# VectorE's order in batch 0, and batch 6's last norm on GpSimd in pieces: one change to a fused attention, feed-forward and gating kernel

## The reference

```python
xn = layernorm(x)
# attention branch
q, k, v = split(xn @ Wqkv + bqkv)
qp, kp  = elu(q) + 1, elu(k) + 1
attn    = (qp @ (kp.T @ v)) / (qp . sum(kp) + 1e-6)
x1 = layernorm(xn + attn) * g1 + b1
s  = layernorm(x1 + (silu(x1 @ Wg + bg) * (x1 @ Wu + bu)) @ Wd + bd) * g2 + b2
# gate branch: three cycles of  out = out + coupling(out) * twist(out)
# coupling: a net of 128-128-64-32-1 with gelu, and one global net on the mean of xn
g  = silu(three cycles on xn)
result = x + s * g
```

## Time and profile before

| what | us |
|---|---|
| median of 3 runs | 166.69 (165.75 to 167.46) |
| the profiled execution | 166.28 |
| its span, first to last instruction | 164.4 |
| busy: TensorE / weight loads | 153.9 / 118.3 |
| busy: VectorE / ScalarE / GpSimd | 138.1 / 132.0 / 111.9 |

### The profile page before, as it was taken

How to read it: one execution, slowest core, us unless ns; L and a number is a source line. 1 busy time by engine, 2 the same in 40 slices (tenths; PEclk the granted TensorE clock), 3 DMA queues, 4 the chain that set the end, 5 groups by cost and what they waited for, 6 DMA issues and landing times.

```text
span 164.4 us, 3402 instructions
## 1 busy us (share of the span) xinstructions
PE 153.9 (94%) x934; PEld 118.3 (72%) x934; DVE 138.1 (84%) x550; ACT 132.0 (80%) x345; POOL 111.9 (68%) x197
## 2 busy tenths in 40 slices
PE   7979999999999999999999999999999999999910
PEld 7757888888898686545554655788888888888910
DVE  2888599899988989299999959968749999969892
ACT  4889876999999988999999986994568887653950
POOL 0075966789991869992084396389999998794352
PEclk9999999999999999999999999999999999999995
DMA  5997333030330000000000000000001011010113
GB/s 173 234 395 161 64 66 68 0 66 7 63 64 0 2 2 4 0 0 0 4 0 0 4 4 0 0 0 4 0 0 66 0 64 63 6 66 0 64 64 128
DMA packets 11922, 7.83 MB, mean 48 GB/s; under 512 B 8960, under 2 KB 9728, under 8 KB 11904
## 3 DMA queue, kind: packets, MB, share of 16 engines
q1 hardware_dynamic: 11616, 7.55, 16.4%
q10 hardware_dynamic: 288, 0.08, 0.2%
HBM read 3.43 MB, written 2.10 MB: 34 GB/s over the span
## 4 chain that ended last, share of the span: by engine, by line
PE 75%; ACT 9%; DVE 8%; POOL 3%; issue 3%; DVEq 0%; ACTq 0%
PE bank L1055 11%; PE bank L1247 10%; PE bank L1172 7%; PE bank L1236 7%; PE bank L1238 7%; PE bank L1237 7%; PE bank L1184 4%; PE bank L1197 4%; PE bank L1126 2%; PE bank L1137 2%; PE bank L1072 2%; PE bank L1113 2%; PE bank L1117 2%; PE bank L1114 2%; DVE u L710 2%
## 5 line engine op out<-in xcount | busy, mean ns | idle before, releaser
L505 ACT ACTIVATE pq<-bank,bffn 128x512 f32<-128x512 f32 (+1 forms) x24 | 16.1, 683 | 11.4 <-PE bank L1238 11.3
L273 POOL TENSOR_TENSOR rstd<-ve,minus_half 128x4 f32<-128x4 f32 x21 | 21.2, 1011 | 1.8
L800 DVE SCALAR_TENSOR_TENSOR pq<-bank,bffn,pq 128x512 f32<-128x512 f32 (+1 forms) x24 | 17.6, 738 | 4.8 <-issue 1.9
L1236 PE MATMUL bank<-x_hi,ffn_hi 128*128 128x512 f32 (+1 forms) x48 | 20.5, 427 | 0.0
L1237 PE MATMUL bank<-x_lo,ffn_hi 128*128 128x512 f32 (+1 forms) x48 | 18.9, 394 | 0.0
L1238 PE MATMUL bank<-x_hi,ffn_lo 128*128 128x512 f32 (+1 forms) x48 | 18.9, 394 | 0.0
L1247 PEld LDWEIGHTS bank<-wd,pq 128*128 128x128 f32 x144 | 17.9, 191 | 1.2
L1247 PE MATMUL bank<-wd,pq 128*128 128x128 f32 x144 | 18.0, 274 | 0.0
L445 ACT ACTIVATE q_stage<-bank,col 128x512 f32<-128x512 f32 x24 | 16.0, 677 | 0.4 <-PE bank L1055 0.3
L271 POOL TENSOR_SCALAR nm<-mv 128x4 f32<-128x4 f32 x21 | 4.7, 223 | 16.5 <-DVE mv L637 16.3
L327 POOL TENSOR_TENSOR ab<-cpl 128x8 f32<-128x8 f32 x4 | 6.5, 1632 | 12.3 <-ACT cpl L477 12.2
(11 more groups left out here) (173 smaller groups left out, 458.2 us busy)
## 6 DMA issues: line engine op xcount, KB each, us to landing
x_tok<-in_x SPq DMA_DIRECT2D x8, 256.0 KB, 6.5
tx_tok<-xn_tok SPq DMA_DIRECT2D x16, 128.0 KB, 2.3
out<-pq SPq DMA_DIRECT2D x7, 256.0 KB, 2.0
r_tok<-in_w_ffn SPq DMA_DIRECT2D x1, 341.0 KB, 6.4
r_tok<-in_w_first SPq DMA_DIRECT2D x1, 320.0 KB, 3.3
out<-pq SPq DMA_DIRECT2D x2, 128.0 KB, 1.9
row<-in_rows SPq DMA_DIRECT2D x1, 192.0 KB, 5.9
wd<-in_w_down SPq DMA_DIRECT2D x1, 192.0 KB, 6.4
```

Of the source, the lines that this page charges most:

```text
L273: return pool.tensor_tensor(rstd[i][:, b], ve[i][:, b], minus_half[:], ALU.pow)
L505: act.activation(sg[n % 2][0:m], gate_of(n)[0:m], ACT.Silu, bias=bffn[0:m, c:c + 1]).then_inc(sg_ready, 1)
L800: dve.scalar_tensor_tensor(out=hid[b % 2][0:m, c], in0=up_of(n)[0:m], scalar=bffn[0:m, CHUNKS + c:CHUNKS + c + 1], in1=sg[n % 2][0:m], op0 ...
L1236: pe.matmul(dst[0:m], ffn_hi[:, w], x1_hi[:, b], start=True, stop=False)
```

## The change

It does six things.

1. VectorE, batch 0: three tiles of batch 2's statistics come first, then `feature_q(0)`, the first `feature_k`, the fourth tile, and the aggregation. The copies and column instructions, now in `small_columns`, stand behind the second `feature_k`.
2. 1/std of batch 6 is no longer made by ScalarE's root and VectorE's reciprocal and product (`rstd_6` is gone) but by GpSimd's power, as for the other batches.
3. ScalarE runs `norm_2(5)` ahead of the silu of the last chunk, and the first root of batch 7 ahead of `norm_2(6)`.
4. `norm_2(6)` signals after tiles 0, 1 and 3.
5. GpSimd's product of batch 6 is made for tile 0, tile 1 and then tiles 2 and 3 together, its sum by halves.
6. The store of batch 6 moves from SyncE to the end of ScalarE's list.

The diff, cut to its core:

```diff
-            b = BATCHES - 2
-            sp.wait_ge(y_ready, b + 1)
-            sp.dma_start(out_dram[b], yb[b % 2]).then_inc(y_stored[b % 2], 16)
...
-            for b in (BATCHES - 3, BATCHES - 2):
-                multiply_rows(b)
-                add_rows_to(b)
+            b = BATCHES - 3
+            pool.wait_ge(y_ready, b)
+            pool.wait_ge(mn_ready, BATCHES)
+            pool.wait_ge(y_stored[b % 2], 16 * (b // 2))
+            link(multiply_rows(b, range(TILES), b + 1))
+            add_rows_to(b, range(TILES)).then_inc(y_ready, 1)
+            rstd_of(2, b + 1)
+            b = BATCHES - 2
+            pool.wait_ge(y_stored[b % 2], 16 * (b // 2))
+            multiply_rows(b, (0,), b + 1)
+            link(multiply_rows(b, (1,), b + 2))
+            add_rows_to(b, HALVES[0]).then_inc(y6_half, 1)
+            link(multiply_rows(b, HALVES[1], b + 3))
+            add_rows_to(b, HALVES[1]).then_inc(y_ready, 1)
...
             def norm_2(b):
-                if b == BATCHES - 2:
-                    act.wait_ge(late_ready, 1)
-                else:
-                    act.wait_ge(rstd_ready[2], b + 1)
+                act.wait_ge(rstd_ready[2], b + 1)
...
+                    if b == BATCHES - 2 and t < 2:
+                        last.then_inc(un_ready, 1)
...
+                if b == BATCHES - 1:
+                    norm_2(b - 2)
                 silu_gate(CHUNKS * b + 2)
...
-                if b >= 2:
+                if 2 <= b < BATCHES - 1:
                     norm_2(b - 2)
...
-            root(BATCHES - 2, range(TILES), 0)
+            root(BATCHES - 1, HALVES[0], 0)
             norm_2(BATCHES - 2)
-            for half, tiles in enumerate(HALVES):
-                root(BATCHES - 1, tiles, half)
+            root(BATCHES - 1, HALVES[1], 1)
+            b = BATCHES - 2
+            act.wait_ge(y6_half, 1)
+            act.wait_ge(y_ready, b + 1)
+            act.dma_start(out_dram[b], yb[b % 2]).then_inc(y_stored[b % 2], 16)
...
-            measure_part(2, HALVES[0])
+            measure_part(2, (0, 1, 2))
...
                 if b == 0:
-                    measure_part(2, (2,))
+                    measure_part(2, (3,)).then_inc(st_ready[0], 1)
+                    moments(0, 2)
...
                 if b == 0:
-                    measure_part(2, (3,)).then_inc(st_ready[0], 1)
+                    small_columns()
...
             residual_last(0)
-            rstd_6()
             measure_last(0)
```

More of the change, by code:

```diff
@@ L206, in gated_block @@
         g_ready, mn_ready, y_ready = sem("g_ready"), sem("mn_ready"), sem("y_ready")
-        y_last, multiplied, root_ready, late_ready = [
-            sem(n) for n in ("y_last", "multiplied", "root_ready", "late_ready")]
+        y_last, y6_half, root_ready, late_ready = [
+            sem(n) for n in ("y_last", "y6_half", "root_ready", "late_ready")]
         y_stored = [sem("y_stored0"), sem("y_stored1")]
@@ L284, in rstd_of, with multiply_rows, add_rows_to @@
                 pool.tensor_tensor(nmr[i][:, b], nm[i][:, b], rstd[i][:, b], ALU.mult).then_inc(rstd_ready[i], 1)
[L286 to L297, removed]
+            def multiply_rows(b, tiles, wanted):
+                pool.wait_ge(un_ready, wanted)
+                ts = slice(tiles[0], tiles[-1] + 1)
+                return pool.tensor_tensor(yb[b % 2][:, ts], un[b % 2][:, ts], tx_tok[:, b, ts], ALU.mult)
+            def add_rows_to(b, tiles):
+                ts = slice(tiles[0], tiles[-1] + 1)
+                return pool.tensor_tensor(yb[b % 2][:, ts], yb[b % 2][:, ts], x_tok[:, b, ts], ALU.add)
             def norm_x1(b):
@@ L828, in residual_6 @@
                     last.then_inc(st_ready[2], 1)
[L830 to L835, removed]
             def rstd_last(half):
@@ L840, in rstd_last @@
                 ts = slice(tiles[0], tiles[-1] + 1)
-                dve.wait_ge(root_ready, 2 + half)
+                dve.wait_ge(root_ready, 1 + half)
                 dve.reciprocal(rstd[2][:, b, ts], std[:, b % 2, ts]).then_inc(late_ready, 1)
@@ L882, in finish_last @@
                 dve.wait_ge(centred, half + 1)
-                dve.wait_ge(late_ready, 2 + half)
+                dve.wait_ge(late_ready, 1 + half)
                 for t in HALVES[half]:
@@ L896, in bias_rows, with small_columns @@
                 last.then_inc(mix_ready, 1)
+            def small_columns():
+                bias_rows()
+                dve.tensor_scalar(half_b4[:], col[:, COL["cn_b4"]:COL["cn_b4"] + 1], 0.5, None, ALU.mult)
+                dve.tensor_scalar(half_gb3[:], col[:, COL["gc_b3"]:COL["gc_b3"] + 1], 0.5, None, ALU.mult)
+                dve.tensor_scalar(gain[:, 0:1], col[:, COL["range"]:COL["range"] + 1], W_GLOBAL, None, ALU.mult)
+                dve.tensor_scalar(gain[:, 1:2], col[:, COL["range"]:COL["range"] + 1], W_TOKEN, None,
+                                  ALU.mult).then_inc(cols_ready, 1)
             def add_rows():
@@ L967, in _ @@
                 if b == 0:
-                    moments(0, 2)
                     lo_x(1)
```

## The result

The changed kernel took 165.22 us (median of 20 runs, 164.82 to 166.44) beside 166.38 us for the one before. The ratio is 0.9942 with a 95% interval of 0.9924 to 0.996: by the ratio 0.97 us less (0.67 to 1.26), where 0.65 was forecast. (The two medians by themselves are 1.16 us apart.) The profiled execution took 165.06 us with a span of 163.2, against 166.28 and 164.4.

What follows compares the result with a forecast made beforehand. TensorE was taken to bound the kernel nearly everywhere except the start and the last 10 us. Head 0.3 plus tail 0.35 gave 0.65 us off, 165.63 or 166.04, so 165.8 was forecast, range 164.9 to 166.9.

Steps and rivals of the forecast that it cites:

- Head: Batch 0's new VectorE order lets TensorE reach batch 2's transposes earlier: 0.3 us gain, bounds 0.45 and a loss of 0.1.
- what is late next is kf of tile 5: Behind batch 2's transposes, TensorE would wait for VectorE's kf of tile 5, losing 0.1 us of the head's gain.
- Travels to the end whole: From the head to 152 us everything hangs on TensorE or its followers, so 0.3 us should reach the end.
- The late silu costs VectorE's row 0.23: Tail: norm of batch 5 first makes the last silu 0.77 us late, costing VectorE's row 0.23.
- rstd leaves VectorE: Tail: without batch 6's rstd 0.95 us goes from VectorE, so its row ends 0.72 earlier net.
- GpSimd takes 1.83 us for the power: Tail: GpSimd makes batch 6's rstd in 1.83 us, so batch 6's norm starts 0.6 us late.
- The pieces: Tail: GpSimd's five pieces for batch 6 cost 0.46 us per 128 columns and 0.73 per 256.
- The store: Tail: batch 6's store, issued by ScalarE, lands at 163.57 against 163.92 for the last landing before; gain 0.35 us.
- Rival (1): GpSimd's pieces are cheap and kf doesn't hold: head 0.4, tail 0.95, 1.35 us off, 165.1; chance 0.12.
- Rival (2): The head gives nothing, kf or ScalarE's copies already setting the pace: 0.35 us off, 166.1; chance 0.18.
- Rival (3): Slower: GpSimd's five pieces and batch 6's store set the end, one piece held 1.4 us: 167.2; chance 0.10.
- the sum would stay as it is: Tail: the new order has no contending VectorE and GpSimd pair, and this was said to leave the 0.65 us unchanged.

Runs made afterwards that it cites:

- e7: Kernel before with batch 2's statistics moved forward in batch 0, but copies and column instructions left ahead of them: ratio 0.9984.
- e1: Kernel before with only VectorE's new order in batch 0, the tail unchanged: ratio 0.997.
- e3: Changed kernel with 1/std of batch 6 again by ScalarE's root and VectorE's reciprocal and product: ratio 0.9914 to the kernel before.
- e2: Changed kernel with batch 0's VectorE order put back, all edits of the tail kept: ratio 0.996 to the kernel before.
- e6: Changed kernel with batch 6's store issued by SyncE again, between the two half stores of batch 7: ratio 0.9979 to the kernel before.
- e9: Kernel before with one edit, the norm of batch 5 ahead of the last silu: ratio 0.9957.
- e4: Changed kernel with the norm of batch 5 put back behind the last silu: ratio 1.0034 to the kernel before.
- e11: Changed kernel with batch 6's 1/std by root and reciprocal, run a second time: ratio 0.9864 to the kernel before.

## Why the prediction was right, and where it was not

The direction, the range and both places were right; the size was 0.65 us for a measured 0.97 (0.67 to 1.26 by the interval), 0.94 by the profile. The range, 164.9 to 166.9, proves little: the 166.38 of the kernel before lies in it too. It is the terms that tell.

- *Head, 0.3 us forecast, 0.42 measured.* The failed step is "what is late next is kf of tile 5". TensorE sums tile n - 2 in the step of tile n, so the load at 18.17 was that of tile 4, whose kf VectorE had begun at 16.75 and so had long written (the row of before is below this list). There was nothing to wait for, and the bound of 0.45 was nearly reached. The cover named for the columns was there; that moving them bought nothing, as e7 shows, the working did not say.
- *Travels to the end whole.* Right: 0.40 at the transposes of e1, 0.44 at its last silu.
- *The late silu costs VectorE's row 0.23.* Too high. I count from the silu before the last (148.73 after; 149.47 before, at the same moment as L271 in the earlier trace rows). The hidden product starts 4.18 behind it instead of 3.50, which is 0.68 later, near the 0.77 of the working. But L833 starts 4.84 behind it (153.57 - 148.73) instead of 4.77 (154.24 - 149.47): it waited for TensorE before, and that wait took up the rest. Cost: 0.07.
- *rstd leaves VectorE, "0.95 us goes".* The size on VectorE's row was right in sum (its last step is 0.78 earlier), the cause was wrong. I booked 0.72 us net to the move of the rstd. e3 shows that with the two instructions back the row ends only 0.05 later. From batch 7's first residual to its statistics were 1.48 us before (157.05 - 155.57), 0.74 in e3 and 0.52 in the changed kernel. Of the 0.96 that went, 0.59 was L834's wait for GpSimd (0.75 against 0.16), and 0.15 was the wait of the reciprocal for a root that came late (from the residual to the reciprocal were 0.59 us before, 156.16 - 155.57, and 0.44 in e3, 155.06 - 154.62). The early norm takes both away by itself. Only 0.22 belongs to the two instructions, and half of that fits into a wait for TensorE. The contention itself I had read correctly, and I had even written that GpSimd's rows of batch 5 would be over by 155.7, but I did not draw the consequence that the root would then have been cheap where it was.
- *GpSimd takes 1.83 us for the power; norm of batch 6 0.6 us later.* Right as a time for the power: 155.01 to 156.84 is 1.83. The norm came 0.45 later (156.87 - 148.73 = 8.14 behind the silu before the last, against 7.69), since the late silu cost less. But the power is a price, and the comparison that matters is with a root that finds GpSimd idle: from the start of batch 6's aggregation to its norm are 2.33 us in the changed kernel (156.87 - 154.54) and 1.15 in e3 (155.47 - 154.32). Of these 1.18 us the differences in the table show 0.58 to 0.68 at the end.
- *The pieces.* 0.46 and 0.73 from the line between 4 and 512 columns; measured 0.454, 0.722 and 0.724 on average. The last piece ended at 160.66, which is 11.93 us behind the silu before the last, against 12.07 in the working (161.54 - 149.47).
- *The store.* Forecast gain of the tail 0.35, measured 0.43 at the last landing (163.92 - 149.47 = 14.45 behind the silu before the last, and 162.75 - 148.73 = 14.02) and 0.52 in e2's difference. The mechanism is e6's: the place in SyncE's queue.

The row of before for the first of these points, from its timeline of VectorE:

```profile
16.75 0.28 DVE L687 SCALAR_TENSOR_TENSOR kf<-ek,bank 128x128 f32<-128x128 f32 x1
```

Rival (1) had kf not holding, which came, but not its cheap pieces. Rival (2) fell with e1. Rival (3) fell with the rows: no piece was held in any of the seven profiles that have pieces. The rule of the Trainium skill ("SBUF — State Buffer", Who interferes with whom), that a VectorE instruction with two SBUF inputs contends with a GpSimd instruction that reads SBUF, is borne out: 0.75 us (before) and 0.76 (e1) beside a GpSimd sum, 0.16 and 0.16 (e3, e9) without one. I had said that by this rule "the sum would stay as it is". It did not: the 0.59 us of the pair are more than the 0.52 that the whole tail gained.

What stays open: what the stops at the start are (last section), and whether the kernels have a part in them. It was not tried. The changed kernel alone gave 8.83 and 9.08 for its first projection.

## What to carry to other kernels

When a tiny instruction is long in a trace, look first for the neighbour that ends when it ends, and price the edit that moves the neighbour away by itself: here two moved lines (0.68 us) did as much as the rewritten tail (0.52), and undoing one part of the rewrite gained another 0.6. Compare a new way of making a value with the old one as it would run after the other edits, not as it ran before them. Time saved on an engine counts only to the next wait it has in common with another engine. To know which tile a load belongs to, count the loop's lag, not the row's position.

## What the runs showed of the hardware

The start scatters more than the change is worth, and the scatter has a row. In e4 TensorE's weight loads of the first weights stand still three times for 0.30 or 0.31 us, and a fourth time for 0.18, with "issue" as the reason, that is, waiting for nothing that the profile shows. In e11 there is no such stop:

```profile
4.84 0.50 PEld L1064 LDWEIGHTS bank<-r_tok 128*128 128x128 f32 x2 [0.31 <-issue]
...
6.50 0.34 PEld L1068 LDWEIGHTS bank<-r_tok 128*128 128x128 f32 x1 [0.30 <-issue]
7.14 0.21 PEld L1068 LDWEIGHTS bank<-r_tok 128*128 128x128 f32 x1 [0.30 <-issue]
```

```profile
4.52 0.30 PEld L1077 LDWEIGHTS bank<-r_tok 128*128 128x128 f32 x2
...
5.86 0.30 PEld L1081 LDWEIGHTS bank<-r_tok 128*128 128x128 f32 x2 [0.59 <-ACT r_tok L547]
```

The first projection began at 9.52 in the one and at 8.46 in the other, and up to there the edits leave TensorE's instructions alone. Over all 13 profiles there are none to four such stops ahead of it, of 0.16 to 0.31 us each. The first projection goes from 8.46 to 9.52, and less the sum of its stops only from 8.39 to 8.61. What the stops are, no run shows. A span from a single profile is therefore no measure of an edit of half a microsecond; the distance between two landmarks behind the start was the same within 0.05 us in the two profiles of each kernel that was run twice (154.37 and 154.32, 153.69 and 153.74).

The time of an execution scatters outside its span as well. Over 89 executions of the kernel before it was 1.77 to 3.07 us longer than the span, so a ratio from few executions carries this scatter too: one and the same kernel gave 0.9914 (e3) and 0.9864 (e11).
